# Four graph layers on one core: one row per node by its last edge, products made before the gather, running values row by row

## What is computed

```python
# layer 0: graph convolution
coef = inv_sqrt_out[src] * inv_sqrt_in[dst]
agg0 = segment_sum((x @ W)[src] * coef[:, None], dst) + b
# layer 1: twice (a, b), each followed by leaky_relu
msg = x[src] @ W_msg + edge_attr @ W_edge
c = where(isneginf(segment_max(msg, dst)), 0, segment_max(msg, dst)) + x @ W_root + b
# layer 2: softmax aggregation, by feature
m = relu(x[src]) + 1e-7
a = exp(m - segment_max(m)[dst]) / segment_sum(exp(m - segment_max(m)[dst]), dst)[dst]
out2 = (x + segment_sum(a * m, dst)) @ W + b
# layer 3: attention with self loops, one score per edge
e = leaky_relu((h @ att_src)[src] + (h @ att_dst)[dst], 0.2)   # h = x @ W
out3 = tanh(segment_sum(h[src] * softmax_by_dst(e), dst) + bias)
```

## Time and profile before

| | us |
|---|---|
| median of 3 runs | 5427.97 |
| lowest, highest | 5404.59, 5431.95 |
| the profiled execution, span | 5313.3 |
| PE busy, weight loads | 3222.1, 2578.5 |
| DVE busy | 3742.5 |
| ACT busy | 2565.5 |
| POOL busy | 3265.5 |

### The profile page before, as it was taken

How to read it: one execution, slowest core, us unless ns; L and a number is a source line. 1 busy time by engine, 2 the same in 40 slices (tenths; PEclk the granted TensorE clock), 3 DMA queues, 4 the chain that set the end, 5 groups by cost and what they waited for, 6 DMA issues and landing times. The chain is left out here.

```text
span 5313.3 us, 65383 instructions
## 1 busy us (share of the span) xinstructions
PE 3222.1 (61%) x14728; PEld 2578.5 (49%) x14728; DVE 3742.5 (70%) x10898; ACT 2565.5 (48%) x4956; POOL 3265.5 (61%) x2855
## 2 busy tenths in 40 slices
PE   3344226666657777566666456556664866776664
PEld 1122126666645555444455356555553655555553
DVE  4465348888846676566667699999995866766665
ACT  0000015545535555455556566666663655555554
POOL 7677345555445666445554577777764777777776
PEclk7676655555568888777777666666665555555555
DMA  5444776666557777566666233333333322222221
GB/s 111 100 93 97 51 90 174 169 165 172 161 151 226 229 237 230 167 177 183 178 182 179 69 101 110 100 98 101 110 97 74 73 67 63 64 72 62 64 70 39
DMA packets 596466, 658.31 MB, mean 124 GB/s; under 512 B 251637, under 2 KB 520151, under 8 KB 596406
## 3 DMA queue, kind: packets, MB, share of 16 engines
q1 hardware_dynamic: 451112, 527.29, 32.1%
q0 software_dynamic: 87808, 128.37, 12.8%
q10 hardware_dynamic: 57486, 2.01, 2.5%
HBM read 431.63 MB, written 252.08 MB: 129 GB/s over the span
## 5 line engine op out<-in xcount | busy, mean ns | idle before, releaser
L433 POOL DMA_INDIRECT l_G<-t,l_idx x784 | 998.1, 1273 | 301.9 <-issue 222.8
L569 POOL DMA_INDIRECT l_gs<-xa,l_idx x392 | 394.7, 1007 | 439.1 <-DMA l_idx<-ids 257.0
L433 POOL DMA_INDIRECT l1b_G<-tc,l1b_idx x392 | 372.9, 951 | 381.4 <-PE l1b_psT L441 214.4
L433 POOL DMA_INDIRECT l1a_G<-t,l1a_idx x392 | 402.7, 1027 | 320.4 <-DMA l1a_idx<-src_rows 152.0
L1575 POOL DMA_INDIRECT out<-l_s_out,l_sidx x392 | 466.4, 1190 | 191.5 <-issue 115.2
L441 PE MATMUL l_psT<-ident,l_G 128*96 128x128 f32 x784 | 187.3, 419 | 640.2 <-DMA l_G<-t,l_idx 623.6
L433 POOL DMA_INDIRECT G<-x_pad,idx x392 | 422.6, 1078 | 170.4 <-issue 130.5
L441 PEld LDWEIGHTS l_psT<-ident,l_G 128*96 128x96 f32 x784 | 141.3, 194 | 670.0 <-DMA l_G<-t,l_idx 354.0
L394 PE MATMUL counts<-hot_lo,hot_hi 128*98 128x512 bf16 x784 | 238.6, 472 | 353.4 <-DVE hot_hi L333 220.3
L330 DVE TENSOR_SCALAR hot_lo<-iota_lo,lo 128x512 bf16<-128x512 f16 x784 | 238.0, 378 | 265.0 <-remote 231.7
L1775 PE MATMUL l_psA<-l_wt,l_T 97*128 97x97 f32 x784 | 298.8, 481 | 115.3 <-ACT l_e_out L1706 93.1
(11 more groups left out here) (272 smaller groups left out, 10146.4 us busy)
## 6 DMA issues: line engine op xcount, KB each, us to landing
t<-l1b_normal SPq DMA_DIRECT2D x98, 384.0 KB
l_xs<-t SPq DMA_DIRECT2D x98, 384.0 KB
xa<-x_pad SPq DMA_DIRECT2D x49, 384.0 KB
xd<-G SPq DMA_DIRECT2D x49, 384.0 KB
l_xn<-x_pad SPq DMA_DIRECT2D x49, 384.0 KB
l_xd_in<-xd SPq DMA_DIRECT2D x49, 384.0 KB
t<-l_xn_out SPq DMA_DIRECT2D x49, 384.0 KB
t<-l_xe_out SPq DMA_DIRECT2D x49, 384.0 KB
```

The source lines that it names most:

```text
L433: pool.indirect_dma_start(tile[:, u, q, :], None, table, bass.IndirectOffsetOnAxis(idx[:, u, q:q + 1], 0)).then_inc(done[u], 16)
L569: pool.indirect_dma_start(gs[:, u, q, :], None, xa, bass.IndirectOffsetOnAxis(idx[:, u, q:q + 1], 0))\
```

## The change

Nearly the whole program is written anew. What it does:

- The hardware loops go; every step of every engine is written out.
- `numbering` gives each node one row: the row of its last edge, or, for a node without an edge, a row that no last edge takes. It is made by one-hot products (one [128x392] and one [128x128] one-hot per edge column, 392 of them) and 27 rounds of shifts and selects over 392 columns on DVE. Partition p now owns the 392 consecutive edges p*392 to p*392+391 (K = 392); a chunk is eight columns of each partition.
- `entry` gathers x by the node of each row into O, a [128 x 393 x 96] tensor that stays in SBUF and holds the residual through all layers; counts out degrees and the row number of each source node by two more passes of one-hots; then writes y0 = (x @ W0) * inv_sqrt_out with a count and the row number as two more columns.
- Each layer gathers rows of a table that the layer before has stored already multiplied: t1, t2 (96 columns), t3 (192: exp(m) and m*exp(m)), t4 (96 products and two scores). The running sum or maximum over edges of one node is a chain of eight dependent [128x96] instructions on DVE a chunk, each with a drain. The running rows are stored to DRAM (hist), and each partition's first segment, which may go on from the partition before, is mended at the end as an extra chunk of one tile (FIX).
- There is no node pass any more. The last row of a node feeds join, norm, the products for the next table and the root product.

Parts of the diff that the steps of the prediction need (all lines are new):

```diff
+# numbering, DVE
+            for c in range(NCH):
+                for q in range(Q):
+                    dve.tensor_scalar(hot_lo[:, c % 2, q, :], k.iota_lo[:, :],
+                                      lo[:, c * Q + q:c * Q + q + 1], None, ALU.is_equal)
+                    made = dve.tensor_scalar(hot_hi[:, c % 2, q, :], k.iota_hi[:, :],
+                                             hi[:, c * Q + q:c * Q + q + 1], None, ALU.is_equal)
...
+# entry, second pass of one-hots, DVE
+                            dve.tensor_scalar(hot_hi[:, u, 0, q, :], k.iota_hi[:, :], hi[:, at],
+                                              rid_hi[:, at], ALU.is_equal, ALU.mult)
...
+# every layer, POOL (SLOTS = 4, in layer 2 it is 3)
+            for c in range(NCH):
+                s = c % SLOTS
+                if c >= SLOTS:
+                    pool.wait_ge(joined, c - SLOTS + 1)
+                    pool.wait_ge(kept[s], 16 * (c // SLOTS))
+                for q in range(Q):
+                    at = c * Q + q
+                    pool.indirect_dma_start(G[:, s, q, :], None, table,
+                                            bass.IndirectOffsetOnAxis(k.src[:, at:at + 1], 0))\
+                        .then_inc(gathered[s], 16)
...
+# layer 0, DVE: the chain, and the order of a step
+                        before = S[:, q - 1, 0:ROW] if q else tile(c - 1)[:, Q - 1, 0:ROW]
+                        done = dve.scalar_tensor_tensor(S[:, q, 0:ROW], before, k.cont[:, at:at + 1],
+                                                        S[:, q, 0:ROW], ALU.mult, ALU.add)
+                        if q < Q - 1:
+                            dve.drain()
...
+            for t in range(LAST + 1):
+                factors(t - 2); chain(t); join(t - 1); take(t - 4)
...
+# layer 1a and 1b, DVE: chain waits for the edge products, join ends a step
+                dve.wait_ge(gathered[c % SLOTS], 128 * (c // SLOTS + 1))
+                dve.wait_ge(edged, 2 * c + 2)
+                dve.tensor_tensor(S, S, E[:, :, 0:D], ALU.add).then_inc(added, 1)
...
+# layer 1a, PE: the order of a step; edges(t) waits for added(t - 1), turn_rows(t - 1) for joined
+                edges(t); multiply(t - 2); turn_rows(t - 1)
...
+# layer 1b, DVE: the order of a step; factors waits for rooted
+                factors(t - 2); weigh(t - 3); chain(t); join(t - 1)
...
+# layer 1b and layer 2, ACT: root
+                act.wait_ge(measured, c + 1)
+                act.activation(lg[:, u, 0:n], mv[:, u, 0:n, 1], ACT.Ln, bias=k.eps[:, :])
+                act.drain()
+                act.activation(rstd[:, u, 0:n], lg[:, u, 0:n], ACT.Exp, scale=-0.5).then_inc(rooted, 1)
...
+# layer 2, ACT: invert is Ln, drain, Exp over [128x768]; the order of a step
+                apply(t - 3); copy_x(t - 4); take(t - 5); invert(t); copy_v(t - 1); root(t - 2)
+# layer 2, DVE
+                factors(t - 3); chain(t); join(t - 1); measure(t - 2); take_own(t - 5)
...
+# layer 3, DVE, ACT and POOL: the orders of a step
+                measure(t - 3); score(t); chain(t - 1); weigh(t - 1); join(t - 2); factors(t - 4)
+                apply(t - 4); exps(t); tanh(t - 2); mix(t - 1); root(t - 3)
+                gather(t); scatter(t - 5)
```

More of the change, by code:

```diff
@@ L46 @@
 LEAK_ATT = 0.2
[L47 to L69, removed]
@@ L99, in tile_columns, with __init__, sem @@
[L99 to L118, removed]
+assert N_NODES == N_EDGES and NCH * Q == K and K < 1 << BITS
+class Kept:
+    pass
+class Stage(ExitStack):
+    def __init__(self, nc):
+        super().__init__()
+        self.nc, self.sems = nc, []
+    def sem(self, name):
+        self.sems.append(self.enter_context(self.nc.semaphore(name)))
+        return self.sems[-1]
@@ new lines, in root, with apply @@
+            def root(c):
+                u, n = c % 2, tiles(c)
+                act.wait_ge(measured, c + 1)
+                act.activation(lg[:, u, 0:n], mv[:, u, 0:n, 1], ACT.Ln, bias=k.eps[:, :])
+                act.drain()
+                act.activation(rstd[:, u, 0:n], lg[:, u, 0:n], ACT.Exp, scale=-0.5).then_inc(rooted, 1)
+            def apply(c):
+                act.wait_ge(factored, c + 1)
+                own = lambda q: k.O[:, c * Q + q, :]
+                norm_apply(act, own, own, rstd, shift, c % 2, tiles(c)).then_inc(normed, 1)
@@ L1710, in root, with exps @@
-            def root(c, i, u, warm):
+            def exps(c):
+                u = c % 2
+                act.wait_ge(scored, c + 1)
+                if c >= 2:
+                    act.wait_ge(weighed, c - 1)
+                act.activation(ex[:, u, :, :], dd[:, u, :, :], ACT.Exp).then_inc(exped, 1)
+                act.drain()
+                for q in range(Q):
+                    last = act.activation(tile(c)[:, q, 0:W3], tile(c)[:, q, 0:W3], ACT.Copy,
+                                          scale=ex[:, u, 1, q:q + 1])
+                last.then_inc(scaled, 1)
@@ L1727, in take_own @@
-            def take_own(c, i, u, warm):
-                act.wait_ge(own_ready, c + 1)
-                if warm:
-                    act.wait_ge(lessened, c - 1)
-                act.activation(own[:, u, :], Hp[:, :, D], ACT.Copy).then_inc(own_out, 1)
-            chunks(act, (join, 3), (scale, 3), (copy, 0), (own_rows, 2), (apply, 5), (exps, 1), (tanh, 3),
-                   (take, 0), (root, 4), (take_own, 2))
+                norm_apply(act, lambda q: e_out[:, c % 3, q, :], lambda q: k.O[:, c * Q + q, :], rstd, shift, u, n)\
+                    .then_inc(normed, 1)
```

2720 lines of the change are left out of this document (1411 added, 1309 removed).

## The result

The changed kernel took 5628.06 us (median of 4 runs, 5623.05 to 5634.67) beside 5429.49 us of the kernel before: ratio 1.038, 95% interval 1.036 to 1.041. The forecast was 4990. Its profiled execution took 5623.05 us and has a span of 5621.2. In all executions of both kernels whose span is on record, time and span differ by only 1.7 to 2.5 us. So the 114.7 us that I carried over are no part of an execution: the profiled execution of the kernel before (span 5313.3) was a faster one than the three whose times were given, as far as the numbers tell.

What follows compares the result with a forecast made beforehand. No engine is full over the whole span; serial loops through in-order queues bind, above POOL's floor of 3439 us. Seven stages sum to 4874 us of span, with 114.7 carried over 4990 us; range 4620 to 5400.

Steps and rivals of the forecast that it cites:

- the 114.7 us: Whole kernel: the median shown stood 114.7 us above the profiled span, and this was added to the forecast span.
- the part on the entry: Entry: gathers, 590 us at most, lie beside DVE's longer one-hot path of 540 us; then y rows 181; 725 us.
- rival E: All stages: the earlier stalls are code fetch, and a straight program fetches all its code; 1480 us more, 6470; chance 0.06.
- Rival C: Layers: DVE and POOL block each other, every transfer 1.273 + 0.30 us; 5335 us; chance 0.10.
- Rival D: Layer 2: 768-byte rows cost two transfers on POOL, 17.4 us, 3.4 more a cycle; 5155 us; chance 0.06.
- The serial loops: Gather layers: the forecast itself, serial loops through the in-order queues bind; 4990 us; chance 0.50.
- Layer 1b: Layer 1b: DVE 11.5 us, idle 3.2 for ACT's root with two table loads, contention 0.5; cycle 15.2, stage 792 us.
- The rule about one table set for both functions: ACT's root: the skill names one set holding Ln and Exp, needing no switch; the forecast assumed separate loads of 1.283 us.

Runs made afterwards that it cites:

- e3: Changed kernel with GpSimd waiting for the landing after each eight gathers in the entry and in layers 0 and 3; 4873.39 us, ratio 0.915 to the kernel before.
- g1: Changed kernel with waits after each eight gathers in entry and all gathering loops, layer 2's logarithms paired, layer 1b's factors after its chain; 4723.85 us, ratio 0.878.
- e5: Changed kernel with GpSimd waiting for the landing after every 16 gathers of the entry only, second chip; 4580.28 us, ratio 0.955 to the kernel before.
- f1: The changed kernel itself, run again on the third chip; 5622.81 us, ratio 1.035 to the kernel before.
- f3: Changed kernel with a GpSimd drain and memset, instead of a landing wait, after each eight gathers of the entry, third chip; 5193.68 us.
- e1: Changed kernel with GpSimd waiting for the landing after each eight gathers of the entry only; 5143.95 us, ratio 0.966 to the kernel before.
- e4: Changed kernel with the entry's 392 gathers replaced by plain DMAs of the same size from ScalarE's queue; 5131.68 us.
- g2: Changed kernel with the entry's 392 gathers replaced by plain DMAs of the same size from GpSimd's own queue, unbroken; 5163.32 us.
- e6: Changed kernel with a GpSimd drain and memset, instead of a landing wait, after each eight gathers of the entry, second chip; 4590.15 us.
- g4: Changed kernel with GpSimd waiting for the landing after every 16 gathers of the entry only, fourth chip; 5611.09 us.
- f2: Kernel before with GpSimd waiting for the landing after each eight gathers in its degrees stage, third chip; 5602.48 us, ratio 1.029 to the kernel before.
- g3: Changed kernel with the first pass of one-hots by SCALAR_TENSOR_TENSOR with a second SBUF input of ones, gathers unbroken; 5549.11 us.

## Why the prediction was wrong

| stage | forecast | changed kernel | e3 | g1 | e5, chip without starvation |
|---|---|---|---|---|---|
| numbering | 243 | 223 | 223 | 223 | 223 |
| entry | 725 | 1124 | 683 | 688 | 680 |
| layer 0 | 580 | 793 | 677 | 677 | 545 |
| layer 1a | 662 | 664 | 664 | 642 | 640 |
| layer 1b | 792 | 702 | 701 | 659 | 679 |
| layer 2 | 744 | 774 | 772 | 678 | 768 |
| layer 3 | 1128 | 1341 | 1153 | 1154 | 1048 |

- **The step that failed** is in the part on the entry and in rival E: the stalls of the earlier trace rows were put down to the loop's turn, and so to something that a straight program leaves behind. They are starvation by POOL's rows, and the change makes more of these: 392 gathers with nothing to wait for in the entry, and in layer 0 a cycle that is POOL's own. The entry was priced as two jobs side by side, with 15 to 17% for contention; beside the gathers DVE's column of 0.40 us took 2.8. Pauses took back 441, 116 and 188 us in the three stages (e3 against the changed kernel on its own chip), 745 of the 747 that the sum was short, though parts cancel in that. Within one chip it is 431 us for the entry (f1 against f3), and 104 and 169 for layers 0 and 3 (e1 against e3). Layer 0 keeps 97 us over its forecast, as the pause is 1.8 to 4.6 us a chunk and stands on POOL, which sets that stage's pace.
- **Rival E** had the sign and the evidence to look for, long idle with no releaser inside a stage, which is there. Its cause isn't: six packets of code beside 35 stalls, and straight code ran freely beside plain copies (e4, g2). So its sign was right by luck, and its time, 6470, was not. Its chance of 0.06 rested on "the 17 stalls stand only ahead of a chunk's first one-hot". That holds for one line of the list; ACT in layers 1a and 1b of the same trace had 193.9 and 190.7 us of "remote", which it does not mention.
- **Rival C** fell: the gathers of layers 0 and 3 have means of 950 and 956 ns in the changed kernel, below the 1273 of the earlier trace rows. **Rival D** fell: the 768-byte gather of layer 2 has 961.

```profile
L733 POOL DMA_INDIRECT l_G<-y,src x392 | 372.4, 950 | 951.3 <-POOLq L414 600.3
L1290 POOL DMA_INDIRECT l_G<-t,src x392 | 376.7, 961 | 348.6 <-DVE l_inv L1338 203.2
L1586 POOL DMA_INDIRECT l_G<-t,src x392 | 374.9, 956 | 188.5 <-issue 118.5
```

- **The serial loops** (A) were right where nothing starved. Layer 1a: 664 against 662. Layer 2: 14.7 us a chunk against 14.0, its four table loads a chunk are there. Layer 3, on the chip without starvation: 21.5 us a chunk against 21.8. Without starvation layer 0 ran at 10.2 against 10.8, and a column of the second one-hots took 0.68 against 0.71 (0.82 with contention).
- **Layer 1b** was over-priced by 90 us. Both table loads a chunk are there, but only one is on the path. ACT's timeline, changed kernel:

```profile
3004.49 0.30 ACT L1110 ACTIVATE l1b_lg<-l1b_mv,eps 128x8 f32<-128x8 f32 x1 [4.79 <-DVE l1b_mv L106]
3004.84 1.28 ACT L1112 ACT_TABLE_LOAD   x1
3006.13 0.21 ACT L1112 ACTIVATE l1b_rstd<-l1b_lg 128x8 f32<-128x8 f32 x1
...
3011.51 1.28 ACT L1110 ACT_TABLE_LOAD   x1
3017.62 0.30 ACT L1110 ACTIVATE l1b_lg<-l1b_mv,eps 128x8 f32<-128x8 f32 x1 [4.83 <-DVE l1b_mv L106]
```

The load for the logarithm runs at 3011.5, ahead of the wait for DVE, in idle time. So the root costs 1.9 us of DVE's time, not 3.2, and the cycle is 13.1, not 15.2. That is 1.3 of the 2.1 us; the other 0.8 was not traced. The rule about one table set for both functions found no support here: each Ln and each Exp had its own load as long as they alternated. Putting the two logarithms of layer 2 side by side (g1) cut that stage by 94 us. The prediction misread here: the load at L1285 belongs to the logarithm of the sums, and the root's own logarithm, L1290, has none ahead of it. The kernel before had the two logarithms side by side already, with two loads a chunk; the change broke that order.
- **The 114.7 us** were the distance between two executions of the kernel before, not between a span and its time, which is 2 us. Without them the forecast is 4876, and the result is 752 us above it. Two slips of the sum are small: 540 + 181 is 721, not 725, and 17 stalls in 49 chunks are one in 2.9, which makes 102 in rival E, not 109.
- The forecast of the span, 4874, is what e3 has (4874.1). With +97 and -90 in it that is luck to the last digit. The stages one by one (1a within 2 us, 2 within 4%, 1b 13% too high) say that most of the work was priced rightly and the interplay wasn't.

## What to carry to other kernels

Idle time with no releaser is read on all engines: look at what GpSimd does at both its ends before giving it a cause. In a straight row of indirect transfers beside engines with many small instructions, try a wait for the landing (some 2 us) after each eight, and measure it, since a pause doesn't always cure, and where GpSimd is what sets the pace (the degrees stage of the kernel before) it costs 2 to 3%. Ask of each stall that a change removes who was working in it.

## What the runs showed of the hardware

- On three of the four chips of the experiments, and on that of the result, which the record does not name, a row of GpSimd's indirect DMAs at one each 1.25 to 1.39 us starved PE, ACT and DVE: 1.4 us between instructions instead of 0.2, 5 to 10 us for a semaphore, whole stalls of up to 21.9 us (23.7 in the kernel before). It ended 3 us after a row of 16, and 27 us after the row of 393. On the second chip it did not starve them. The kernel before was 10 to 12% faster there, e6 12% faster than the same program on the third chip (f3), and e5 18% faster than on the fourth (g4). How the engines are starved, and why chips differ, stays open. The fetch of code is excluded as sole cause by e1, f2 and the six packets, the traffic by e4 and by the 24 us without any, and the port lock by layer 0, where ACT still waits from 1697 to 1705 us, while DVE does nothing. Every execution here was also recorded, so whether recording has a part in it is not known. The changed kernel itself was never run on the second chip. That it would be faster than the kernel before there is inferred from e5 (0.955), which differs by the pauses in the entry alone.
- Indirect form and row length both matter: plain DMAs of the same size from the same queue, one each 0.70 us, starved nobody; rows of 8 starved nobody in the changed kernel, but held up ACT by some 4 us a chunk in layers 1a and 1b of the kernel before; in the entry rows of 16 starved as much as the row of 393, in layer 3 rows of 16 starved nobody, and an unbroken row at one each 1.47 us (g3, second pass) starved nobody.
- In the other direction, gapless one-hots on VectorE held up one GpSimd transfer for 89 us (g2), 218 us (f2) and 311 us (g3), to the end of the pass. Not always: beside the equally gapless second pass of g3 no gather took over 1.5 us. What decides it was not tested.
- A table load is placed right behind the last function of the old set and runs ahead of the semaphore wait of the one that needs it, at 1.283 us, so it is free wherever ACT has idle time there.
